# One exchange of the score maxima per half, and scores one quad further ahead, in a fused attention and expert kernel

## What is computed

```python
x = x + xattn(layernorm(x), ctx, ctx)          # ctx: (32, 1601, 256)

def xattn(query, key, value):                  # 16 attention heads of width 16
    q = split_heads(query @ Wq.T + bq)
    k = split_heads(key @ Wk.T + bk)
    v = split_heads(value @ Wv.T + bv)
    score = einsum('bhqd,bhkd->bhqk', q, k) * SCALE
    attn = softmax(score, axis=-1)
    out = einsum('bhqk,bhkd->bhqd', attn, v)
    return merge_heads(out) @ Wp.T + bp
```

## Time and profile before

| what | value |
| --- | --- |
| median of 3 runs | 1787.09 us (1785.63 to 1788.38) |
| profiled execution | 1784.61 us |
| its span, first to last instruction | 1782.8 us |
| mean granted TensorE clock over the span | 0.98 |
| busy over the span: PE, DVE, ACT, POOL | 96%, 81%, 68%, 53% |

### The profile page before, as it was taken

How to read it: one execution, slowest core, us unless ns; L and a number is a source line. 1 busy time by engine, 2 the same in 40 slices (tenths; PEclk the granted TensorE clock), 3 DMA queues, 4 the chain that set the end, 5 groups by cost and what they waited for, 6 DMA issues and landing times. The chain is left out here.

```text
span 1782.8 us, 60648 instructions
## 1 busy us (share of the span) xinstructions
PE 1714.3 (96%) x24916; PEld 1388.7 (78%) x24916; DVE 1443.7 (81%) x3380; ACT 1214.0 (68%) x3361; POOL 947.5 (53%) x1427
## 2 busy tenths in 40 slices
PE   7999999999999999999999999998599799999998
PEld 4777777777777777777777777776477799999998
DVE  5788888888888888888888888888785767666667
ACT  4687777777777777777877778777555356666652
POOL 5345555555455565555554555543411338888850
PEclk9999999999999999999999999998699899999999
DMA  4111111111111111111111111121102336666633
GB/s 172 32 52 44 63 47 41 66 44 61 49 41 66 44 44 66 41 48 62 44 62 45 47 63 44 44 66 59 40 33 83 124 142 223 222 217 228 216 122 114
DMA packets 43444, 147.96 MB, mean 83 GB/s; under 512 B 5680, under 2 KB 25008, under 8 KB 39712
## 3 DMA queue, kind: packets, MB, share of 16 engines
q1 hardware_dynamic: 38416, 130.72, 21.5%
q0 software_dynamic: 4752, 13.38, 2.4%
HBM read 129.79 MB, written 14.16 MB: 81 GB/s over the span
## 5 line engine op out<-in xcount | busy, mean ns | idle before, releaser
L500 ACT ACTIVATE a_probs<-a_probs,a_bias 128x401 f32<-128x401 f32 x1024 | 635.9, 626 | 0.0
L725 DVE TENSOR_SCALAR_CACHE_REDUCE a_probs<-a_pss 128x401 f32<-128x401 f32 x1024 | 523.2, 564 | 17.1 <-POOL a_sums L341 1.4
L740 DVE STREAM_TRANSPOSE a_pT<-a_probs 128x1664 f32<-128x1664 f32 x256 | 487.8, 1906 | 35.3 <-ACT a_probs L500 25.7
L975 PE MATMUL a_pss<-a_keys,a_qown 32*32 32x401 f32 x8192 | 313.4, 509 | 2.9 <-DVE a_probs L725 2.2
L339 POOL TENSOR_SCALAR a_ex<-a_probs,a_marks 128x4 f32<-128x4 f32 x256 | 76.1, 297 | 389.3 <-ACT a_probs L500 386.4
L316 POOL TENSOR_TENSOR a_clo<-a_raw,a_chi 128x416 fp32r<-128x416 f32 x240 | 251.4, 1081 | 0.0
L1010 PE MATMUL a_pso<-a_pT,a_v 128*32 128x128 f32 x6656 | 214.3, 280 | 0.7 <-DVE a_pT L740 0.7
L1010 PEld LDWEIGHTS a_pso<-a_pT,a_v 128*32 128x32 f32 x6656 | 179.5, 112 | 33.0 <-issue 27.3
L500 ACT ACTIVATION_READ_ACCUMULATOR a_probs<-a_probs,a_bias 128x1 f32 x1024 | 197.0, 192 | 0.0
L1681 PE MATMUL e_psg<-e_xh,e_guh 128*128 128x256 f32 x660 | 189.7, 287 | 5.5 <-DVE e_hl L1427 4.0
L1682 PE MATMUL e_psg<-e_xl,e_guh 128*128 128x256 f32 x660 | 186.6, 283 | 0.0
(11 more groups left out here) (253 smaller groups left out, 4317.7 us busy)
## 6 DMA issues: line engine op xcount, KB each, us to landing
a_raw<-in_ctxT SPq DMA_DIRECT2D x60, 832.0 KB, 4.5
f_gur<-in_wgu SPq DMA_DIRECT2D x24, 1408.0 KB, 6.1
f_dr<-in_wd SPq DMA_DIRECT2D x24, 768.0 KB, 4.7
e_big<-ys_scr SPq DMA_DIRECT2D x8, 512.0 KB, 6.7
a_probs<-in_ctxT SPq DMA_DIRECT2D x2, 1664.0 KB, 9.0
a_x<-in_x SPq DMA_DIRECT2D x16, 128.0 KB, 4.5
rows_scr<-f_a SPq DMA_DIRECT2D x8, 256.0 KB, 2.3
rows_scr<-f_a SPq DMA_DIRECT2D x4, 512.0 KB, 3.5
```

What stands on the lines that cost most here:

```text
L500: nc.scalar.activation(z, z, ACT.Exp, bias=bias[:, group % 4, at_bias:at_bias + 1], scale=-1.0, accum_out=esum[:, h % 2, j, 2 * e + r:2 * ...
L725: nc.vector.tensor_scalar(probs[:, at % RING, j, 0:KG], ps_s[:, j, 0:KG], -SCALE, None, ALU.mult, ALU.min, accum_out=nmax[:, group % 2, at ...
L740: nc.vector.transpose(pT[:, turned_slot(h, i)].rearrange("p j k -> p (j k)"), probs[:, at % RING].rearrange("p j k -> p (j k)")).then_inc( ...
L975: mm = nc.tensor.matmul(ps_s[32 * g:32 * g + 32, j, 0:KG], q_own[32 * j:32 * j + 32, n % 2, m, e, 32 * r:32 * r + 32], keys[32 * j:32 * j ...
```

## The change

- `turn_max`, `reduce_max`, `spread_max` and `copy_bias` work on a whole half, 16 units, and stand once in a period, not twice: on PE the turn follows the scores at the start of the third quarter, and the spread stands after the first step behind it; on DVE the reduction follows the third turn; on ACT the copy stands ahead of the exponentials of the next half's first quad. `bias` has two slots of 16 columns in place of four slots of 8.
- PE makes scores one quad earlier: quads 2 and 3 of half `h + 1`, then quads 0 and 1 of half `h + 2`. DVE takes quads 1, 2, 3 of half `h + 1` and quad 0 of half `h + 2`.
- The ring `probs` has six slots, `pT` five. Quads of odd halves are turned in another order, and the wait for the weighted sums of the half before stands at the second turn.
- `weigh` does its 13 tiles in one piece, in the first quarter, ahead of the step there.
- In odd halves step 9 is moved from the first quarter to the second.
- ACT no longer splits the exponentials of quads 1, 2 and 3 into pairs.

The diff, cut to these parts:

```diff
-RING, TURNED = 5, 6
+RING, TURNED = 6, 5
 def quads(h):
-    return ((1, 0), (1, 1), (0, 0), (0, 1)) if h % 3 == 1 else ((0, 0), (0, 1), (1, 0), (1, 1))
+    return ((1, 1), (0, 0), (0, 1), (1, 0)) if h % 2 else ((0, 0), (0, 1), (1, 0), (1, 1))
 def turned_slot(h, i):
-    return (i, (4, 5, 0, 1)[i], 2 + i)[h % 3]
+    return 4 if h % 2 and i == 0 else i
 def steps_in(h):
-        plan = [[(n + 1, 9)], [(n + 1, 10), (n + 1, 11)], [(n + 1, 12), (n + 1, 13)], [(n + 1, 14), (n + 2, 0)]]
+        plan = [[], [(n + 1, 9), (n + 1, 10), (n + 1, 11)], [(n + 1, 12), (n + 1, 13)], [(n + 1, 14), (n + 2, 0)]]
...
# ACT
             def period(h):
                 steps = steps_in(h)
                 if h >= 0:
-                    exponentials(h, 1, FORMER)
-                    copy_bias(2 * h + 1)
-                    exponentials(h, 1, LATTER)
+                    exponentials(h, 1)
                 copy_steps(steps[0])
...
                 if h >= 0:
-                    exponentials(h, 2, FORMER)
-                copy_steps(steps[1][:1])
+                    exponentials(h, 2)
...
+                copy_steps(steps[1])
...
-                if h + 1 < NH:
-                    copy_bias(2 * h + 2)
                 if h >= 0:
-                    exponentials(h, 3, FORMER)
...
+                    exponentials(h, 3)
...
+                copy_steps(steps[2])
                 if h + 1 < NH:
+                    copy_bias(h + 1)
                     exponentials(h + 1, 0, FORMER)
...
# DVE
             def turn(h, i):
-                if i >= 2 and h > 0:
+                if i == 1 and h > 0:
                     dve.wait_ge(o_filled, h)
...
             def period(h):
                 for i in range(HALF):
+                    taken = (h + 1, i + 1) if i < HALF - 1 else (h + 2, 0)
                     if i == 2 and h > 0:
                         if h + 1 < NH:
-                            dve.wait_ge(s_filled, HALF * (HALF * (h + 1) + i) + 1)
+                            dve.wait_ge(s_filled, HALF * (HALF * (h + 1) + 3) + 1)
                         invert(h - 1)
-                    if h + 1 < NH:
-                        take_scores(h + 1, i)
+                    if taken[0] < NH:
+                        take_scores(*taken)
                     if h >= 0:
                         turn(h, i)
-                    if i % 2 == 1 and h + 1 < NH:
-                        reduce_max(2 * (h + 1) + i // 2)
                     if i == 1 and h % 4 == 1 and h > 4:
                         residual(h // 4 - 1)
+                    if i == 2 and h + 1 < NH:
+                        reduce_max(h + 1)
...
+            take_scores(0, 0)
             for h in range(-1, NH):
                 period(h)
...
# PE
-            def weigh(h, some):
+            def weigh(h):
...
+            scores(0, 1)
             def period(h):
                 steps = steps_in(h)
                 if h + 1 < NH:
-                    scores(h + 1, 1)
-                if h >= 0:
-                    spread_max(2 * h + 1)
+                    scores(h + 1, 2)
+                if h > 0:
+                    weigh(h - 1)
                 for z in steps[0]:
                     step(*z)
-                if h > 0:
-                    weigh(h - 1, range(FIRST_TILES))
                 if h > 0:
                     total(h - 1)
                 if h + 1 < NH:
-                    scores(h + 1, 2)
-                for z in steps[1][:1]:
-                    step(*z)
+                    scores(h + 1, 3)
                 if h % 4 == 1 and h > 4:
                     project_out(h // 4 - 1)
-                if h + 1 < NH:
-                    turn_max(2 * h + 2)
-                for z in steps[1][1:]:
-                    step(*z)
-                if h > 0:
-                    weigh(h - 1, range(FIRST_TILES, KT))
-                if h + 1 < NH:
-                    scores(h + 1, 3)
-                    if h % 4 == 1 and h > 4:
-                        pe.wait_ge(x1_ready, h // 4)
-                    spread_max(2 * h + 2)
-                for z in steps[2]:
+                for z in steps[1]:
                     step(*z)
                 if h + 2 < NH:
                     scores(h + 2, 0)
+                if h + 1 < NH:
+                    if h % 4 == 1 and h > 4:
+                        pe.wait_ge(x1_ready, h // 4)
+                    turn_max(h + 1)
+                for z in steps[2][:1]:
+                    step(*z)
+                if h + 1 < NH:
+                    spread_max(h + 1)
+                for z in steps[2][1:]:
+                    step(*z)
+                if h + 2 < NH:
+                    scores(h + 2, 1)
                 for z in steps[3][:1]:
                     step(*z)
                 if h > 0:
                     spread(h - 1)
-                if h + 1 < NH:
-                    turn_max(2 * h + 3)
                 for z in steps[3][1:]:
                     step(*z)
```

More of the change, by code:

```diff
@@ L494, in exponentials, with copy_bias @@
                 e, r = quads(h)[i]
-                group = 2 * h + i // 2
-                act.wait_ge(bias_ready, group + 1)
+                act.wait_ge(bias_ready, h + 1)
                 for j in some:
                     z = probs[:, at % RING, j, 0:KG]
-                    at_bias = HALF * (i % 2) + j
-                    nc.scalar.activation(z, z, ACT.Exp, bias=bias[:, group % 4, at_bias:at_bias + 1], scale=-1.0,
+                    at_bias = HALF * i + j
+                    nc.scalar.activation(z, z, ACT.Exp, bias=bias[:, h % 2, at_bias:at_bias + 1], scale=-1.0,
                                          accum_out=esum[:, h % 2, j, 2 * e + r:2 * e + r + 1]).then_inc(exp_done, 1)
-            def copy_bias(group):
-                act.wait_ge(max_spread, group + 1)
-                nc.scalar.copy(bias[:, group % 4, :], ps_m[:, P:P + 2 * HALF]).then_inc(bias_ready, 1)
+            def copy_bias(h):
+                act.wait_ge(max_spread, h + 1)
+                nc.scalar.copy(bias[:, h % 2, :], ps_m[:, P:P + HALF * HALF]).then_inc(bias_ready, 1)
             def copy_out(h):
@@ L989, in spread_max @@
+            def spread_max(h):
+                pe.wait_ge(max_reduced, h + 1)
                 for g in range(QK):
-                    mm = nc.tensor.matmul(ps_m[32 * g:32 * g + 32, P:P + 2 * HALF], lowest[:, group % 2, :], a_id_sb[0:2 * HALF, 0:2 * HALF], start=True, stop=True)
+                    mm = nc.tensor.matmul(ps_m[32 * g:32 * g + 32, P:P + HALF * HALF], lowest[:, h % 2, :], a_id_sb[0:HALF * HALF, 0:HALF * HALF],
+                                          start=True, stop=True)
                 mm.then_inc(max_spread, 1)
-            def weigh(h, some):
+            def weigh(h):
@@ L995, in weigh @@
                 n, m = h // 2, h % 2
-                if some.start == 0:
-                    pe.wait_ge(turned, HALF * (h + 1))
-                    pe.wait_ge(kv_copied, STEPS * (n + 1))
-                    if h > 0:
-                        pe.wait_ge(o_copied, h)
-                for t in some:
+                pe.wait_ge(turned, HALF * (h + 1))
+                pe.wait_ge(kv_copied, STEPS * (n + 1))
+                if h > 0:
+                    pe.wait_ge(o_copied, h)
+                for t in range(KT):
@@ L1011, in weigh @@
-                if some.stop == KT:
-                    mm.then_inc(o_filled, 1)
+                        mm = nc.tensor.matmul(ps_o[32 * j:32 * j + 32, 0:P], v_of(n)[:, t, 32 * p:32 * p + 32],
+                                              pT[:, h % 2:h % 2 + HALF, j, 32 * t:32 * t + 32], start=(t == 0), stop=(t == KT - 1))
+                mm.then_inc(o_filled, 1)
             def total(h):
                 pe.wait_ge(sums_ready, HALF * (h + 1))
-                pe.wait_ge(max_ready, min(HALF * (HALF * (h + 2) + 1) + 1, HALF * HALF * NH))
+                pe.wait_ge(max_ready, min(HALF * (HALF * (h + 2) + 2) + 1, HALF * HALF * NH))
@@ L1031, in project_out @@
                 pe.wait_ge(o_ready, 4 * t + 4)
-                pe.wait_ge(bias_ready, min(8 * t + 12, 2 * NH))
+                pe.wait_ge(bias_ready, min(4 * t + 6, NH))
                 for e in range(NC):
@@ L1137, in _ @@
                     total(NH - 1)
-                    weigh(NH - 1, range(KT))
+                    weigh(NH - 1)
                     pe.wait_ge(loaded, 16 * 7)
```

41 lines of the change are left out of this document (11 added, 30 removed).

## The result

The changed kernel takes 1746.55 us (median, 1745.66 to 1749.71) against 1787.74 (1785.63 to 1790.88) for the kernel before beside it: a ratio of 0.977, with a 95% interval from 0.975 to 0.979, or 41 us. The forecast was 1742. The profiled execution's span went from 1782.8 to 1743.9, 38.9 less; the mean granted clock is 0.98 as before.

A forecast was written before the change was run, and what follows sets the result against it. PE's queue was taken to set the pace, losing 0.73 us a half waiting for DVE. Terms -0.73, -0.31, -0.10, 0, +0.40 gave -0.74 a half, -44 over 59 halves, -45 with the ends: 1742 us, range 1724 to 1770.

The forecast's parts named there:

- the copy wait: Even halves: scores moved to the third quarter wait 0.80 us for ACT's copy of step 3's keys; +0.40 a half.
- waits for DVE, long quarters: PE's scores in long first and third quarters wait for DVE's takes; these losses go, -0.67 us a half.
- the small ones: Small PE losses of about 0.06 us a half, at quads that start with a lead of 1.9; they go.
- sums in one piece: Weighted sums on PE: one piece costs 2.70 us in place of 3.01 for two; -0.31 a half.
- steps: Odd halves: step 9 joins other steps in a run, saving 0.19 us every second half; -0.10 a half.
- maxima: PE's turn and spread, one each for two: 0.58 us goes, 0.61 comes; 0 a half, between -0.38 and +0.1.
- the walk: PE's and DVE's rows, ACT's order included, laid end to end from an even half's scores: no lead under 1.84 us.
- The threshold: Lead, from DVE's take to PE's scores of the next quad, below which PE pays the difference: 1.84 us.
- The rival of the tile changes: Only tile-mode changes on PE count, 0.19 us each: 31 us less in all, 1756; chance 0.08.
- The first four need no cover: Sums on PE, steps moved, maxima and the new copy wait count in full, since PE has no idle place.
- The slower rival: PE's spread between value steps waits for late ACT exponentials through DVE's reduce: 24 us slower, 1811; chance 0.11.
- Start and end: Takes open once at the start, 1 us more; exponentials wait for maxima once at the end, 2 less; together -1.

The follow-up runs named there:

- the kernel with even and odd steps: Changed kernel with even-half steps two by two over the quarters and odd-half steps as before the change, step 9 in the first quarter: 1747.39 us, ratio 0.978.
- the value step behind: Changed kernel with value step 4 moved from the third to the second quarter of even halves, behind key step 3: 1753.19 us, ratio 0.981.
- steps two by two: Changed kernel with the eight steps of even halves spread two by two over the quarters: 1743.28 us, ratio 0.975.

## Why the prediction was right, and where it was not

The time was forecast to 5 us, and its mechanism held: PE's waits for DVE go, the copy wait comes, and the difference is won in every half. But 0.74 a half was forecast and 0.65 came, and some terms are off in opposite directions, so that the forecast is this close is in part luck. Each was measured anew; by quarters, per half on average:

| term | forecast | measured | from |
| --- | --- | --- | --- |
| waits for DVE, long quarters | -0.67 | -0.67 | (0.99 + 0.99 + 0.68) / 4 in the table of quarters, the same instructions with and without the wait |
| the small ones | -0.06 | -0.12 | fourth quarters, 0.15, 0.06, 0.15 and 0.14 longer before |
| sums in one piece | -0.31 | -0.08 | 2.87 in odd and 2.99 in even halves against 3.01 |
| steps | -0.10 | -0.10 | step 9 put back (half 3 of four, the kernel with even and odd steps against the changed one): first quarter +1.50, of which 0.12 is the sums' new neighbour, second -1.18; so 0.20 in odd halves |
| maxima | 0 | -0.05 | go: 0.36 + 0.11; come: 0.37 + 0.05 |
| copy | +0.40 | +0.40 | 577.81 to 578.90 |
| sum | -0.74 | -0.62 | halves: -0.65 |

By half the same terms give -0.41, -1.12 and -0.52 for h mod 4 = 0 and 2, 1 and 3; the table of quarters has -0.44, -1.16 and -0.57. So 0.03 to 0.05 a half stays unattributed.

*The waits.* Right. No scores of the changed kernel in periods 2 to 59 take over 0.5 us to issue, and leads of 2.3, 2.9, 3.0, 2.9 and 4.3, 2.8, 2.5, 2.8 stand against 2.3, 2.6, 2.6, 2.8 and 4.2, 2.6, 2.6, 2.8 of the walk. Laying the rows end to end was the part of the prediction that carried it. Its quarters came within 0.1 but for the two with the sums, 5.1 and 3.6 there, 5.40 and 3.89 measured; 3.6 had also left out `total`, by its own pieces it is 3.7. Two things in this step were off. The threshold is 2.02, not 1.84: by the spreading of the scores, lead and loss add up to 1.10 + 0.92 with the value step behind, 1.38 + 0.65 with steps two by two, 1.21 + 0.81 with odd steps back. In the kernel before, too, the issue of the scores was spread out by 1.17 more at a lead of 0.84 (1.64 in place of 0.47), 2.01 in sum; but the quarter grew by 0.99 alone. A `spread_max` stood right behind those scores, and the difference is its 0.18, which so seems to lie beside the wait. Where none stood, in fourth quarters with leads of 1.9, a loss of 0.12 was paid that the 1.84 does not show; hence the small ones, 0.12 in place of 0.06. And the cause of the small lead was named too narrowly: the prediction put it to the reduce behind a late `turn_max`, and the turns made early won 11 us, not 29. Two more causes stood behind it, the second piece of the sums, for which turns wait, and quarters of uneven length; each became visible only when the one ahead of it was gone.

*The sums.* The term that was mis-sized most: 0.31 forecast, 0.08 measured. The step that failed was to fit a line through pieces of 64 and 40 instructions. The first is followed by `total`, which has the sums' own tile shape, 128 by 32, the second by scores in another; so the fit took a difference in the piece's tail for a cost per instruction. Measured, 104 instructions take 2.87 ahead of `total` and 2.99 ahead of a step (606.97 to 609.96): the neighbour is worth 0.12, as much as joining the pieces (0.11 in the kernel where only that was done).

*The maxima.* The spread between steps costs 0.37 where 0.56 was taken, between its two bounds. A turn ahead of a step costs 0.11 in one place and nothing in the other (behind `spread`, 0.60 to the step's second product with it and without), where 0.11 was taken for both.

*The rival of the tile changes.* It gave -0.19 for sums, steps and maxima together, the forecast -0.41; measured is -0.23. So on these terms the rival was nearer, which by itself would have given 1756. The time came out 9 us below that: the small waits are 0.06 a half more than forecast, these terms 0.04 more than the rival's, 0.03 a half is unattributed, and the ends gave 0.7. Against the forecast, the sums are 0.23 short and the small waits, the maxima and the rest make up for some 0.14; the 0.09 that is left, 59 times, is the 5 us by which the forecast was off.

*"The first four need no cover."* True of PE, which was never idle there, but not of the parts. That sentence took it that work taken off PE is time won. The sums alone in one piece take work off PE and make the kernel 63 us slower, since they take from a quarter the length that DVE needs. That part is a gain only together with others. The sum of terms was right for it because the walk of leads had shown that no quarter of the whole falls short.

*The copy wait.* Right to the hundredth, and shown by its removal: even halves lost 0.80.

*The slower rival.* Did not occur: from 60 to 1180 us PE has no wait ahead of the spread. At 580.15 the reduce had waited 0.42 for the turn, as the prediction said it would above a lead of some 2.9 (3.0 here). In the rival's own price there is a slip: 2.5 late less 1.3 is 1.2 of waiting, not 1.14, which gives 1814 and not 1811. Turns wait for exponentials once in each half, 22.6 us in 22 halves, 1.0 each as in the walk.

*Start and end.* Forecast +1 and -2, measured +2.2, -5.1 and, behind the first layer, +2.2: -0.7 in all against -1, again by sizes that cancel. At the start the scores of two quads follow each other and wait for takes as forecast, but the clock was lower too, and how much of the 2.2 is the wait is not shown (see the end). From period 60 to the last exponential the six kernels made from the changed one take 60.0 to 61.7, the four made from the kernel before 64.5 to 66.9. So the gain comes with what the latter four lack; that it is the single exchange, as forecast, was not tested apart. The 2.2 behind it lie in the second layer, whose instructions are the same. That stretch takes 529.5 in the kernel before and from 531.3 to 535.1 in the ten experiments, 531.8 in the changed kernel, so the change is not shown to cause them.

Left open: which of the single exchange, the quad further ahead and the sixth slot removes the last waits. They need each other (a quad further ahead needs the slot, and one exchange needs quads taken earlier), and were not separated.

## What to carry to other kernels

Where one set of buffers ties a busy engine to a second one, measure the lead of the second, find the threshold (here 2.02 us; its four takes last 1.98), and walk the rows of both engines end to end through a whole cycle: the sum of the first engine's work decides nothing while one lead falls short. A stretch between two such meetings that is shorter than the second engine's own work (here 4 us) is free only behind one that let the second engine run ahead, and a long stretch lets it only if its inputs come early in it; steps laid by that rule, with the spread and the projection moved, won 23 us beyond the change. A part of a change can be slower by itself and belong to a faster whole, and a price taken from two pieces with different neighbours holds the neighbours too.

## What was not expected of the hardware

The granted clock at the start. Between 40 and 60 us it is 0.91 in the changed kernel; the window of the kernel before:

```profile
40.00:60.00 20.00, 20.00 (x237) 16.50 (x230) 8.28 (x33) 8.32 (x18) 0.00 (x0) 1.00 0.14 44
```

The changed kernel's PE, ahead of that:

```profile
38.28 4.67 PE L965 MATMUL a_pss<-a_keys,a_qown 32*32 32x401 f32 x64 [1.01 <-DVE a_probs L713]
...
43.39 0.55 PE L926 MATMUL a_psk<-a_clo,a_whi 128*128 128x416 f32 x1
```

PE waited unit by unit for DVE's takes, over 4.67 us for 64 instructions, and behind it key products take 0.55 in place of 0.36, at the lower level of 1.2 GHz, until 45.6. The first scores of the next period are 2.8 later (63.22 against 60.38), where 1 was forecast for the start.

That the longer wait made the clock fall is not shown. The kernel before with only its turns made early has, up to there, the instructions of the kernel before, one quad and not two, and its clock falls as well, and for longer, from 41.5 to 48.3:

```profile
39.90 3.02 PE L975 MATMUL a_pss<-a_keys,a_qown 32*32 32x401 f32 x32 [1.01 <-DVE a_probs L725]
...
43.37 0.55 PE L936 MATMUL a_psk<-a_clo,a_whi 128*128 128x416 f32 x1
```

Its first scores of the next period come at 64.22, 3.8 later than in the kernel before. All ten experiments show the fall at this place; of the twelve traces only that of the kernel before does not. So the 2.8 are the wait and the clock together, and the same start was met at either level.

What a piece costs depends on its neighbours, by 0.1 to 0.2, and those here differ in tile shape: the same spread 0.19 beside scores, 0.37 between steps, the same sums 2.87 ahead of `total`, 2.99 ahead of a step.
